# A dense relation layer moved beside a scatter in a graph network kernel

## The chip, the cores and the metric

The kernel runs on one core of a Trainium2 chip. The metric is the device time of one launch in microseconds; the time before is the median of 3 runs.

## What is computed

Four graph layers follow each other on 100,000 nodes of 64 features and 50,000 edges sorted by destination, each with a residual and a layer norm. Each has a part that only nodes reached by an edge need and a dense part for the nodes that no edge reaches:

```python
x = _layernorm(x + L0(x, edge_index, ...))      # graph convolution, two rounds
x = _layernorm(x + L1(x, src, dst, ...))        # attention; without edges: x @ res_W + res_b
x = _layernorm(x + L2(x, edge_attr_64, ...))    # relations; without edges h_nb = 0:
#   out = leaky_relu((nfeat + h_nb) @ res_fc_w.T) + leaky_relu(nfeat * h_nb @ res_fc2_w.T)
x = _layernorm(x + L3(x, src, dst, ...))        # update: mlp([nodes, aggregated])
```

## The kernel before

Nodes are worked in 98 blocks of 1024 (128 partitions by 8 rows), edges ("slots") in 98 blocks of 512. A table in HBM holds slots first and nodes behind them; `x1_table`, `x2_table` and `x3_table` hold the result of the layers. What a node without edges needs is a chain of dense layers over all nodes, attention, relations, update, which the class `Nodes` writes. It is independent of the work on edges, so each dense layer is put beside a stage of the edge work. The stages run one after the other, each in a block of its own with a barrier behind it:

- `own_phase`: gathers each edge's own row (GpSimd), and the dense first layer.
- `slot_phase` (the slot stage): GpSimd writes 392 pieces of `slot_info` into `node_table` with indirect DMAs (L1064) and waits for nothing; beside it the dense attention layer, 98 blocks.
- `first_conv_phase`: 4 gathers a block (L1243), scaling, transposes (L1297), a scan along the edges, a projection (L1304, L1306) and a convolution (L1313); beside it the dense relation layer, 98 blocks.
- `second_conv_phase`: 4 gathers a block (L1424), transposes (L1467), a scan, a sum (L1478, L1480) and its norm; beside it the dense update layer, 98 blocks, whose rows go to the output.
- `attention_phase`, `relation_phase`, `message_phase`: the edge work of the other layers, with no dense layer beside them. The last has 4 gathers (L2380) and 4 scatters a block on GpSimd.

A dense block in `Nodes` goes through these steps: `load` (SP, six buffers, waits until the block six before is transposed), `turn` (TensorE, four transposes, L783, waits for the copy of the block before), `copy` (ScalarE, L861), for relations and update `project` (TensorE, L797 or L794) and `bend` (ScalarE), then `sum_up` (TensorE: L837 and L841 for attention, L845 and L847 for relations, L837, L850 and L853 for update), `squares` (ScalarE, L887), `powers` (VectorE, L914), `roots` (ScalarE, L894), `invert` and `scale_rows` (VectorE), and `store` (SP).

The order on each engine is written by hand: `over_turns` takes a list of stages with their lags, and in turn t each engine issues, in the order of the list, stage (t - lag) of each. An engine waits in order, so what stands behind a waiting instruction waits with it. A TensorE fp32 matmul appears in the profile as two records, a transpose as one.

```python
def over_turns(*stages):
    for turn in range(max(lag + blocks for _, lag, blocks in stages)):
        for stage, lag, blocks in stages:
            if 0 <= turn - lag < blocks:
                stage(turn - lag)
```

## Time and profile before

| | |
|---|---|
| median of 3 runs | 7181.63 us (7180.82 to 7210.08) |
| the profiled execution's own time | 7214.96 us |
| its span | 7213.2 us, mean granted TensorE clock 0.764 |
| TensorE matmul busy | 5373.8 us, 75% |
| VectorE busy | 3019.9 us, 42% |
| ScalarE busy | 1930.0 us, 27% |
| GpSimd busy | 3025.0 us, 42% |

Busy shares are means over seven stages with different limits. The span is that from the first to the last instruction; the execution's own time is the one to set a sum against. PE is TensorE's matmuls, PEld its weight loads, DVE VectorE, ACT ScalarE, POOL GpSimd, SP the engine that issues the plain DMAs. The ends of matmuls are modelled, so when a matmul was really done shows in who waits for it. The granted clock is a share of 2.4 GHz, and is either 1 or 0.5 at any time.

### The profile page before, as it was taken

Reading aid. Unit: us, or ns where it says so; the run is one execution under the profiler, and the core shown is the slowest. Engines: PE = TensorE matmul, PEld = TensorE weight load, DVE = VectorE, ACT = ScalarE, POOL = GpSimd, SP = SyncE. Lnnn points to the kernel's source line nnn. Section 1 sums busy time; section 2 is a strip of 40 time slices with the busy share of each in tenths; the row PEclk is TensorE's granted clock in tenths of the full one; section 3 lists DMA queues with packets and bytes.
Section 4 is the critical chain, followed back from the end, with each engine's and each line's share of the span. In section 5 each row is a group of like instructions: output and inputs, shape, how many; then the busy total and the mean of one; then the engine's idle time right before and its main releaser. Section 6 shows DMA issues by size and latency. Waiting matters only on the chain. (4 is left out here: it accounts for less than half of the span.)

```text
span 7213.2 us, 79067 instructions
## 1 busy us (share of the span) xinstructions
PE 5373.8 (75%) x24847; PEld 3452.0 (48%) x24847; DVE 3019.9 (42%) x5947; ACT 1930.0 (27%) x3627; POOL 3025.0 (42%) x3150
## 2 busy tenths in 40 slices
PE   3888700165888889995578848999999987777776
PEld 2656500144666667773255634444454444444443
DVE  4333300033555535553345526666666642222222
ACT  1333300032333333331111102333343431112121
POOL 2444477501554444445455131222222104666665
PEclk9877755566999989997666559788787857777777
DMA  3666500144666645553344223233232202222221
GB/s 105 191 192 190 163 16 16 28 122 115 168 172 170 156 124 139 137 139 71 71 93 93 64 49 86 72 74 74 72 79 68 68 22 61 52 51 51 52 59 27
DMA packets 1238916, 676.24 MB, mean 94 GB/s; under 512 B 1021942, under 2 KB 1054989, under 8 KB 1238504
## 3 DMA queue, kind: packets, MB, share of 16 engines
q1 hardware_dynamic: 1138152, 582.13, 30.1%
q0 software_dynamic: 100352, 89.06, 6.6%
q8 instruction: 205, 3.36, 0.2%
q14 instruction: 207, 1.70, 0.1%
HBM read 410.58 MB, written 263.03 MB: 93 GB/s over the span
## 5 line engine op out<-in xcount | busy, mean ns | idle before, releaser
L914 DVE TENSOR_REDUCE n_power<-n_square 128x8 f32<-128x512 f32 x392 | 268.9, 686 | 1675.8 <-issue 1069.3
L2075 POOL DMA_INDIRECT r_got<-x_table,slot_idx x392 | 376.9, 961 | 1299.6 <-DVE r_rows L2270 1022.0
L1243 POOL DMA_INDIRECT a_got<-node_table,src_idx x392 | 371.3, 947 | 721.1 <-POOLq L1059 371.3
L887 ACT ACTIVATE n_square<-n_sum_t 128x512 f32<-128x512 f32 x392 | 234.1, 597 | 1317.5 <-remote 567.6
L1424 POOL DMA_INDIRECT b_rows<-h_table,slot_idx x392 | 369.7, 943 | 430.8 <-PE b_rows_t L1467 302.3
L2380 POOL DMA_INDIRECT m_rows<-x_table,slot_idx x392 | 376.7, 961 | 395.8 <-POOLq L2065 276.7
L2388 POOL DMA_INDIRECT out_dram<-s_res,put_out x392 | 390.0, 995 | 338.7 <-DVE s_res L1181 213.2
L952 POOL DMA_INDIRECT o_rows<-in_x_dram,dst_idx x392 | 372.4, 950 | 378.7 <-DVE o_rooted L1032 271.4
L1866 POOL DMA_INDIRECT t_got<-x_table,slot_idx x392 | 372.8, 951 | 362.3 <-DVE t_rows L1984 207.3
L837 PE MATMUL n_sum_t<-res_wide,ones 3*128 3x512 bf16 x98 | 49.7, 507 | 613.0 <-issue 424.5
L2167 PE MATMUL r_source_t<-r_masked,rel_pair 64*128 64x512 f32 x980 | 487.8, 644 | 0.0
L2169 PE MATMUL r_own_t<-r_masked,rel_pair 64*128 64x512 f32 x980 | 487.6, 644 | 0.0
L1141 ACT ACTIVATE s_square<-s_sum_t 128x256 f32<-128x256 f32 x392 | 149.3, 381 | 1246.1 <-remote 523.4
L1064 POOL DMA_INDIRECT node_table<-slot_info,put_slot x392 | 391.1, 998 | 163.5 <-issue 134.0
L2515 DVE TENSOR_TENSOR_SCAN m_both<-m_keep,m_both,m_rows_t 128x512 f32<-128x512 bf16 x97 | 124.1, 1279 | 792.7 <-remote 440.9
L2297 DVE SCALAR_TENSOR_TENSOR r_masked<-r_half,r_both_t 128x512 f32<-128x512 bf16 x490 | 301.2, 681 | 97.8 <-PE r_both_t L2152 69.0
L783 PE MATMUL n_turned_t<-ident,n_rows 128*128 128x128 f32 x1568 | 293.9, 320 | 44.3 <-DMA n_rows<-x_table 33.0
L837 PEld LDWEIGHTS n_sum_t<-res_wide,ones 3*128 3x128 bf16 x98 | 9.4, 96 | 646.3 <-issue 430.5
L861 ACT ACTIVATE n_turned_s<-n_turned_t 128x512 f32<-128x512 f32 x392 | 231.0, 589 | 272.6 <-remote 159.2
L2167 PEld LDWEIGHTS r_source_t<-r_masked,rel_pair 64*128 64x128 f32 x980 | 194.9, 209 | 226.2 <-issue 184.1
L1147 DVE TENSOR_REDUCE s_power<-s_square 128x4 f32<-128x256 f32 x392 | 162.5, 415 | 325.7 <-ACT s_square L1141 262.4
L783 PEld LDWEIGHTS n_turned_t<-ident,n_rows 128*128 128x128 f32 x1568 | 220.5, 166 | 146.7 <-issue 102.1
(362 smaller groups left out, 12834.4 us busy)
## 6 DMA issues: line engine op xcount, KB each, us to landing
n_rows<-x_table SPq DMA_DIRECT2D x294, 256.0 KB
x_table<-n_res SPq DMA_DIRECT2D x196, 256.0 KB
node_table<-n_wide SPq DMA_DIRECT2D x98, 272.0 KB
x_table<-n_res SPq DMA_DIRECT2D x98, 260.0 KB
h_table<-n_conv SPq DMA_DIRECT2D x98, 256.0 KB
x_table<-s_res SPq DMA_DIRECT2D x196, 128.0 KB
r_feats<-in_edge_attr_dram SPq DMA_DIRECT2D x390, 64.0 KB
n_rows<-in_x_dram SPq DMA_DIRECT2D x97, 256.0 KB
```

The costliest lines, as they stand in the source:

```text
L783: last = nc.tensor.transpose(self.turned_t[:, q * P:(q + 1) * P], self.rows[:, n % AHEAD, 2 * q:2 * q + 2, :].rearrange("p j d -> p (j d)" ...
L952: nc.gpsimd.indirect_dma_start(out=rows[:, n % 4, t, :], out_offset=None, in_=x, in_offset=bass.IndirectOffsetOnAxis(ap=dst_idx[:, n * TIL ...
L1064: nc.gpsimd.indirect_dma_start(out=units, out_offset=bass.IndirectOffsetOnAxis(ap=put_slot[:, k:k + 1], axis=0), in_=slot_info[:, k, :], i ...
L1243: nc.gpsimd.indirect_dma_start(out=got[:, n % 4, t, :], out_offset=None, in_=node_table, in_offset=bass.IndirectOffsetOnAxis(ap=src_idx[:, ...
L1424: nc.gpsimd.indirect_dma_start(out=rows[:, n % 4, t, 0:D], out_offset=None, in_=h_table, in_offset=bass.IndirectOffsetOnAxis(ap=slot_idx[: ...
L1866: nc.gpsimd.indirect_dma_start(out=got[:, n % RING, t, :], out_offset=None, in_=x1_table, in_offset=bass.IndirectOffsetOnAxis(ap=slot_idx[ ...
L2075: nc.gpsimd.indirect_dma_start(out=got[:, n % RING, t, :], out_offset=None, in_=x2_table, in_offset=bass.IndirectOffsetOnAxis(ap=slot_idx[ ...
L2167: nc.tensor.matmul(source_t[:, :], rel_pair[0:D, k, :], masked[0:D, n % 2, k, :], start=(k == 0), stop=(k == PAIRS - 1), skip_group_check= ...
L2169: last = nc.tensor.matmul(own_t[:, :], rel_pair[D:P, k, :], masked[D:P, n % 2, k, :], start=False, stop=(k == PAIRS - 1), skip_group_check ...
L2297: nc.vector.scalar_tensor_tensor(out=masked[:, n % 2, k, :], in0=half[:, n % 3, :], scalar=float(k), in1=both_t[:, :], op0=ALU.is_equal, o ...
L2380: nc.gpsimd.indirect_dma_start(out=rows[:, n % 4, t, 0:D], out_offset=None, in_=x3_table, in_offset=bass.IndirectOffsetOnAxis(ap=slot_idx[ ...
L2388: nc.gpsimd.indirect_dma_start(out=out, out_offset=bass.IndirectOffsetOnAxis(ap=put_out[:, n * TILES + t:n * TILES + t + 1], axis=0), in_= ...
```

## The change

The dense relation layer moves from the first convolution into the slot stage, as a second object of `Nodes` named `later` that transposes the attention layer's result rows straight from their buffer in SBUF; its loads from `x2_table` are gone. The dense update layer is halved: blocks 0 to 48 run in the first convolution, 49 to 97 in the second, one block every second turn, with one sum buffer in PSUM. In both convolutions the scan buffer goes from two to three deep, and the edge work behind the scan runs one turn later. The second convolution gets a second buffer for the transposed rows.

```diff
         def turn(self, pe, n):
-            pe.wait_ge(self.loaded[n], self.loaded.done(n))
+            if self.source is None:
+                pe.wait_ge(self.loaded[n], self.loaded.done(n))
+                rows = self.rows[:, n % AHEAD]
+            else:
+                pe.wait_ge(self.source.ready[n], self.source.ready.done(n))
+                rows = self.source.res[:, n % 4]
...
         def scale_rows(self, dve, n):
...
+            if self.reader is not None:
+                if n >= 4:
+                    dve.wait_ge(self.reader.turned[n - 4], self.reader.turned.done(n - 4))
...
     def slot_phase():
             nodes = Nodes(c, "attention")
+            later = Nodes(c, "relations", source=nodes)
...
-                    over_turns((store, AHEAD + 2, BLOCKS), (load, 0, BLOCKS))
+                    over_turns((store_later, AHEAD + 5, BLOCKS), (store, AHEAD + 2, BLOCKS), (load, 0, BLOCKS))
...
-                    over_turns((sum_up, 1, BLOCKS), (turn, 0, BLOCKS))
+                    over_turns((sum_up, 1, BLOCKS), (turn, 0, BLOCKS), (sum_later, 4, BLOCKS), (turn_later, 2, BLOCKS),
+                               (project_later, 3, BLOCKS))
...
-                    over_turns((squares, 1, BLOCKS), (roots, 1, BLOCKS), (copy, 0, BLOCKS))
+                    over_turns((copy, 0, BLOCKS), (squares, 1, BLOCKS), (copy_later, 2, BLOCKS), (squares_later, 4, BLOCKS), (roots, 1, BLOCKS),
+                               (roots_later, 4, BLOCKS), (bend_later, 3, BLOCKS))
...
-                    over_turns((powers, 1, BLOCKS), (invert, 1, BLOCKS), (scale_rows, 1, BLOCKS))
+                    over_turns((powers, 1, BLOCKS), (powers_later, 4, BLOCKS), (invert, 1, BLOCKS), (scale_rows, 1, BLOCKS),
+                               (invert_later, 4, BLOCKS), (scale_later, 4, BLOCKS))
...
+    def every(turns, stage):
+
+        def at_turn(n):
+            if n % turns == 0:
+                stage(n // turns)
+        return at_turn
+
+    EARLIER = BLOCKS // 2
+
     def first_conv_phase():
-            nodes = Nodes(c, "relations")
+            nodes = Nodes(c, "update", 0, EARLIER, sums=1)
...
-            scan = sb(c, "a_scan", [P, 2, EDGE_BLOCK])
+            scan = sb(c, "a_scan", [P, 3, EDGE_BLOCK])
...
-                    over_turns((sum_nodes, 2, BLOCKS), (convolve, 3, BLOCKS), (project_nodes, 1, BLOCKS), (turn, 1, BLOCKS),
-                               (turn_nodes, 0, BLOCKS), (project, 2, BLOCKS))
+                    over_turns((every(2, sum_nodes), 2, BLOCKS), (project, 3, BLOCKS), (every(2, project_nodes), 1, BLOCKS), (convolve, 4, BLOCKS), (turn, 1, BLOCKS),
+                               (every(2, turn_nodes), 0, BLOCKS))
...
     def second_conv_phase():
-            nodes = Nodes(c, "update")
+            nodes = Nodes(c, "update", EARLIER, BLOCKS - EARLIER, sums=1)
...
-            scan = sb(c, "b_scan", [P, 2, EDGE_BLOCK])
-            rows_t = pb(c, "b_rows_t", [P, EDGE_BLOCK])
+            scan = sb(c, "b_scan", [P, 3, EDGE_BLOCK])
+            rows_t = [pb(c, f"b_rows_t{h}", [P, EDGE_BLOCK]) for h in range(2)]
...
-                    over_turns((sum_nodes, 2, BLOCKS), (add_up, 2, BLOCKS), (project_nodes, 1, BLOCKS), (turn, 1, BLOCKS),
-                               (turn_nodes, 0, BLOCKS))
+                    over_turns((every(2, sum_nodes), 2, BLOCKS), (add_up, 3, BLOCKS), (every(2, project_nodes), 1, BLOCKS), (turn, 1, BLOCKS),
+                               (every(2, turn_nodes), 0, BLOCKS))
```

ScalarE, VectorE and SP have the matching lists: the dense update steps at every second turn, the edge steps behind the scan one turn later.

TensorE in the slot stage, one turn and the start of the next, before (the `n_` names are the attention layer's, `ident` the unit matrix for transposes):

```order
L837 MATMUL n_sum_t_2<-res_wide,ones_0 128x512
L841 MATMUL n_sum_t_2<-res_pair,n_turned_s 128x128 x4
L783 MATMUL n_turned_t<-ident,n_rows 128x128 x4
L837 MATMUL n_sum_t_2<-res_wide,ones_0 128x512
L841 MATMUL n_sum_t_2<-res_pair,n_turned_s 128x128 x4
```

and with the change (the `q_` names are the relation layer's):

```order
L850 MATMUL n_sum_t_2<-res_wide,ones_0 128x512
L854 MATMUL n_sum_t_2<-res_pair,n_turned_s 128x128 x4
L796 MATMUL n_turned_t<-ident,n_rows 128x128 x4
L858 MATMUL q_sum_t_2<-slope_pair,q_turned_s 128x128
L860 MATMUL q_sum_t_2<-bent_pair,q_hidden 128x128
...
L796 MATMUL q_turned_t<-ident,n_res 128x128 x4
L810 MATMUL q_hidden_t<-q_turned_s,fc_pair 128x512
L850 MATMUL n_sum_t_2<-res_wide,ones_0 128x512
```

A turn has grown from 9 matmuls and transposes to 22: the relation layer's sum (eight), transposes (four) and projection (one) stand behind the attention layer's transposes.

ScalarE in the slot stage, one turn with the change:

```order
L874 ACTIVATE n_turned_s<-n_turned_t 128x512
L900 ACTIVATE n_square<-n_sum_t_2 128x512
L874 ACTIVATE q_turned_s<-q_turned_t 128x512
L900 ACTIVATE q_square<-q_sum_t_2 128x512
L907 ACTIVATE n_deviation<-n_power,eps 128x8
L907 ACTIVATE q_deviation<-q_power,eps 128x8
L894 ACTIVATE q_hidden<-q_hidden_t 128x512
```

Before, a turn was the square, the root and the copy of the attention layer; the copy now stands ahead, and the bend of the relation layer, on which the next turn's later sum waits, stands last.

## Rows read from the trace of the kernel before

In rows 1 a number in brackets behind a busy time is the count of instructions.

**Rows 1.** Windows view: us; PE, PEld, DVE, ACT, POOL busy (x); PEclk, DMA share, GB/s.

```profile
889.00:1399.00 510.00, 50.79 (x195) 38.47 (x195) 22.13 (x42) 21.51 (x43) 379.38 (x381) 0.51 0.08 17
1422.00:1770.00 348.00, 215.84 (x1049) 163.09 (x1049) 128.00 (x243) 112.04 (x243) 0.00 (x0) 0.71 0.44 119
1810.00:2480.00 670.00, 573.40 (x3319) 429.87 (x3318) 352.10 (x717) 231.42 (x448) 338.30 (x358) 0.93 0.68 169
2570.00:3290.00 720.00, 693.12 (x4487) 524.67 (x4485) 361.75 (x824) 265.51 (x548) 345.34 (x367) 0.96 0.53 134
6000.00:7150.00 1150.00, 850.37 (x3190) 490.16 (x3187) 302.40 (x463) 227.95 (x465) 719.23 (x735) 0.77 0.21 50
```

**Rows 2.** Source view, GpSimd lines: count, ns min/median/max, first and last start us.

```profile
L1064 POOL DMA_INDIRECT node_table<-slot_info,put_slot x392: 981/982/1280, 874.0 to 1398.1; - x196
...
L1243 POOL DMA_INDIRECT a_got<-node_table,src_idx x392: 938/944/1189, 1770.4 to 2490.6; - x196
...
L1424 POOL DMA_INDIRECT b_rows<-h_table,slot_idx x392: 938/944/957, 2528.5 to 3291.1; - x196
...
L2380 POOL DMA_INDIRECT m_rows<-x_table,slot_idx x392: 940/947/1001, 5980.3 to 7166.1; - x196
```

**Rows 3.** Timeline under the scatter: start us, us, instruction, idle before and its releaser.

```profile
1207.86 0.60 PE L837 MATMUL n_sum_t<-res_wide,ones 3*128 3x512 bf16 x1 [33.05 <-issue]
...
1208.39 2.08 PE L841 MATMUL n_sum_t<-res_pair,n_turned_s 128*128 128x128 f32 x8
...
1210.26 1.06 PE L783 MATMUL n_turned_t<-ident,n_rows 128*128 128x128 f32 x4
...
1232.52 0.60 ACT L887 ACTIVATE n_square<-n_sum_t 128x512 f32<-128x512 f32 x1 [24.71 <-remote]
...
1233.15 0.69 DVE L914 TENSOR_REDUCE n_power<-n_square 128x8 f32<-128x512 f32 x1 [34.53 <-issue]
1233.88 0.30 ACT L894 ACTIVATE n_deviation<-n_power,eps 128x8 f32<-128x8 f32 x1 [0.76 <-issue]
...
1243.72 0.60 ACT L861 ACTIVATE n_turned_s<-n_turned_t 128x512 f32<-128x512 f32 x1 [9.55 <-remote]
```

**Rows 4.** Timeline of the slot stage behind the scatter, TensorE at 2.4 GHz.

```profile
1431.31 0.39 PE L837 MATMUL n_sum_t<-res_wide,ones 3*128 3x512 bf16 x1 [1.79 <-ACT n_turned_s L861]
...
1432.62 0.60 PE L783 MATMUL n_turned_t<-ident,n_rows 128*128 128x128 f32 x4
```

**Rows 5.** Timeline of the first convolution, TensorE, one turn.

```profile
2113.31 1.10 PE L1313 MATMUL a_conv_t<-w_cen,a_hidden 128*128 128x64 f32 x8
...
2114.25 1.08 PE L797 MATMUL n_hidden_t<-n_turned_s,fc_pair 128*128 128x512 f32 x2
...
2115.17 0.60 PE L1297 MATMUL a_rows_t<-ident,a_rows 128*128 128x128 f32 x4
...
2116.14 0.38 PE L1304 MATMUL a_hidden_t<-a_root,split 9*128 9x512 bf16 x1
...
2117.41 0.39 PE L845 MATMUL n_sum_t<-slope_pair,n_turned_s 128*128 128x128 f32 x2
...
2119.20 0.98 PE L1313 MATMUL a_conv_t<-w_cen,a_hidden 128*128 128x64 f32 x7
```

**Rows 6.** Timeline of the second convolution, TensorE and GpSimd.

```profile
2905.72 0.38 PE L837 MATMUL n_sum_t<-ub_wide,ones 3*128 3x512 bf16 x1 [0.30 <-issue]
...
2907.76 0.94 POOL L1424 DMA_INDIRECT b_rows<-h_table,slot_idx  x1 [0.30 <-issue]
...
2908.86 0.20 PE L1478 MATMUL s_sum_t<-split,b_root 9*128 9x65 bf16 x1
...
2910.84 1.13 PE L794 MATMUL n_hidden_t<-n_turned_s,u_w 64*128 64x512 f32 x4
...
2911.90 0.66 PE L1467 MATMUL b_rows_t<-ident,b_rows 128*128 128x128 f32 x4
...
2912.83 0.94 POOL L1424 DMA_INDIRECT b_rows<-h_table,slot_idx  x1 [2.88 <-PE b_rows_t L1467]
```

More of the change, by code:

```diff
@@ L698, in build, with __init__ @@
     class Nodes:
-        def __init__(self, c, layer):
-            self.layer = layer
+        def __init__(self, c, layer, first=0, blocks=BLOCKS, source=None, sums=2):
+            self.layer, self.first, self.blocks, self.source, self.reader = layer, first, blocks, source, None
+            if source is not None:
+                source.reader = self
+            tag, of = ("n", "n_") if source is None else ("q", "")
+            of_sums = of or "s_"
             gcn, mlp = layer == "gcn", layer in ("gcn", "update")
-            self.gcn, self.mlp = gcn, mlp
+            self.gcn, self.mlp, self.sum_count = gcn, mlp, sums
@@ L714, in __init__ @@
-            self.sum_t = [pb(c, f"n_sum_t{h}", [P, 2, 512] if gcn else [P, 512]) for h in range(2)]
+            if source is None:
+                self.rows = sb(c, "n_rows", [P, AHEAD, ROWS, D])
+                self.loaded = sig.landing("n_loaded", 1, AHEAD, blocks)
+            self.turned_s = sb(c, f"{tag}_turned_s", [P, 4, 512])
+            self.square = sb(c, f"{tag}_square", [P, 2, ROWS, D])
+            self.power = sb(c, f"{tag}_power", [P, 2, ROWS])
+            self.deviation = sb(c, f"{tag}_deviation", [P, 2, ROWS])
@@ L749, in load @@
             else:
-                table = {"attention": x1_table, "relations": x2_table, "update": x3_table}[self.layer]
-                sp.dma_start(self.rows[:, n % AHEAD], of_nodes(table, n)[:, :, 0:D]).then_inc(self.loaded[n], 16)
+                table = {"attention": x1_table, "update": x3_table}[self.layer]
+                sp.dma_start(self.rows[:, n % AHEAD], of_nodes(table, self.first + n)[:, :, 0:D]).then_inc(self.loaded[n], 16)
         def store_table(self, sp, n):
@@ L1098, in roots, with copy_later, bend_later, squares_later @@
                         nodes.roots(act, n)
-                    over_turns((squares, 1, BLOCKS), (roots, 1, BLOCKS), (copy, 0, BLOCKS))
+                    def copy_later(n):
+                        later.copy(act, n)
+                    def bend_later(n):
+                        later.bend(act, n)
+                    def squares_later(n):
+                        later.squares(act, n)
+                    def roots_later(n):
+                        later.roots(act, n)
+                    over_turns((copy, 0, BLOCKS), (squares, 1, BLOCKS), (copy_later, 2, BLOCKS), (squares_later, 4, BLOCKS), (roots, 1, BLOCKS),
+                               (roots_later, 4, BLOCKS), (bend_later, 3, BLOCKS))
                 @block.vector
@@ L1281, in store_nodes @@
                         nodes.store(sp, n)
[L1282 removed]
+                    over_turns((every(2, store_nodes), 7, BLOCKS), (store, 8, BLOCKS), (load, 0, BLOCKS), (every(2, load_nodes), 0, BLOCKS), (load_rooted, 3, BLOCKS),
                                (by_groups(load_flags), 0, BLOCKS))
@@ L1305, in project @@
                         pe.wait_ge(scanned[n], scanned.done(n))
-                        nc.tensor.matmul(hidden_t[:, :], w1_2[:, :], scan[:, n % 2, :], start=False, stop=True).then_inc(projected[n], 1)
+                        nc.tensor.matmul(hidden_t[:, :], w1_2[:, :], scan[:, n % 3, :], start=False, stop=True).then_inc(projected[n], 1)
                     def convolve(n):
@@ L1453, in store_nodes @@
                         nodes.store(sp, n)
-                    over_turns((store_nodes, 7, BLOCKS), (store, 7, BLOCKS), (load, 0, BLOCKS), (load_nodes, 0, BLOCKS),
+                    over_turns((every(2, store_nodes), 7, BLOCKS), (store, 8, BLOCKS), (load, 0, BLOCKS), (every(2, load_nodes), 0, BLOCKS),
                                (by_groups(load_flags), 0, BLOCKS))
@@ L1479, in add_up @@
                                              skip_group_check=True)
-                            last = nc.tensor.matmul(to[:, t, :], scan[:, n % 2, k], cen2[:, :], start=False, stop=True,
+                            last = nc.tensor.matmul(to[:, t, :], scan[:, n % 3, k], cen2[:, :], start=False, stop=True,
                                                     skip_group_check=True)
```

107 lines of the change are left out of this document (59 added, 48 removed).

## The prediction

> **What bounds the kernel now.** The kernel runs in seven stages, each closed by a barrier, so I read it stage by stage. The windows view comes first [rows 1], with the first and last gather or scatter of each stage beside it [rows 2], then the timeline inside the stages the change touches [rows 3 to 6]. All sums are made against the profiled execution, 7214.96 us with a span of 7213.2 us. The median of the runs is 33.3 us lower, and I subtract that at the end.
>
> The slot stage lasts from 874.0 to 1770.4 us, 896 us [rows 2]. The scatter that GpSimd does ends at 1398.1. The dense attention layer should run beside it, 98 blocks of three VectorE instructions each. But between 1422 and 1770 VectorE still runs 243 of them [rows 1], which is 81 blocks. So only 17 blocks were done in the 548 us before. The stage is scatter, then dense layer, one after the other. The rows say why. In one turn under the scatter TensorE starts the sum at 1207.86 and the transposes at 1210.26, as usual. Yet ScalarE, waiting for the sum, starts only at 1232.52, and for the transposes at 1243.72 [rows 3]. ScalarE and VectorE then follow each other in hundredths of a us. Only what TensorE signals is late, by 22 to 32 us. TensorE completes 195 matmul records in the 510 us from 889 to 1399 [rows 1]: one per 2.6 us, 13 to a turn (1 + 8 + 4 [rows 3]), at a granted clock of 0.51, which is the 1.2 GHz level. Without the scatter a turn takes 348 / 81 = 4.3 us.
>
> The first convolution takes 1770.4 to 2528.5 us. In its steady part there are 358 gathers, four to a block, so 89.5 turns in 670 us, 7.49 us each. TensorE is 86% busy at clock 0.93 [rows 1]. The second takes 720 / (367 / 4) = 7.85 us a turn. TensorE is busy 693.12 us of 720, so it is bound by TensorE. GpSimd is at 5.0 us a turn in both: 0.94 us per gather and 0.30 between them [rows 6].
>
> **The change part by part.**
>
> *Slot stage.* Per block the relation layer adds four transposes, a projection and a sum of eight matmuls. The last two print two records for each matmul [rows 5], so that is 4 + 2 + 16 = 22 TensorE records, and a turn then has 35. If what holds TensorE back goes by records, the scatter covers 195 / 35 = 5.6 turns behind the first two, 8 in all. The bounds of this term are 17 turns, if the delay goes by the turn as now, and 5, if each added wait adds one of its own; with the price of a turn below they move the stage by -49 and +16 us. I take 8, since sum (9 records, 24.7 us) and transposes (4, 11.2 us) come out at the same time per record [rows 3]. VectorE's new wait, for the reader's transposes of four blocks ago, finds them two turns old. If it did hold VectorE, the attention layer's scaling and what is queued behind it would wait, and the reader with them; I cost it at nothing.
>
> What remains is 102 - 8 = 94 turns (98 and a lag of 4) with no scatter beside them. A turn on TensorE at the high clock is: attention sum 1.31 (1431.31 to 1432.62 [rows 4]), transposes twice 0.49 (2115.17 to 2116.14 holds two sets), relation sum 1.79 (2117.41 to 2119.20) and projection 0.92 (2114.25 to 2115.17 [rows 5]), together 5.0 us. The longest loop through the other engines starts at the later layer's sum, which waits for its bend: sum 1.79, transposes 0.49, copy 0.60, squares 0.60, VectorE's sum of squares 0.69, roots 0.30, bend 0.60 [rows 3], 5.07 us and seven handovers of some 0.03. So 5.3 us, and both chains agree. ScalarE has 5 x 0.60 + 2 x 0.30 = 3.6 us of work a turn and VectorE 6 x 0.53 = 3.2 (128.00 us for 243 instructions [rows 1]): neither binds. I take 5.4, for the cold start behind the scatter: 94 x 5.4 = 508 us, the stage ends at 1930 in place of 1770, **+160 us**. SP issues three transfers of 256 KB a turn instead of two. That is 148 GB/s at 5.3 us, where the first convolution moves 169 GB/s [rows 1]: nothing. SP's order (later store, store, load) puts the later store ahead of a load that waits for TensorE anyway.
>
> *First convolution.* TensorE's turn is 5.89 us (2113.31 to 2119.20 [rows 5]). The relation layer in it is 1.79 + 0.49 + 0.92 = 3.20 us. The update layer costs 3.14 for its sum (2905.72 to 2908.86), 1.06 for its projection (2910.84 to 2911.90) [rows 6] and 0.49, together 4.69 us, but every second turn only, 2.35. The turn's TensorE work goes from 5.89 to 5.04 us. The 1.6 us above it (7.49 less 5.89) I take as nearly unchanged: 6.5 us. Bounds: 5.3, TensorE and GpSimd with nothing above them, and 7.2, where the rest grows. 98 x 0.99 = **-97 us**. The three-deep scan buffer and the convolve one turn later remove a wait of TensorE on VectorE that this order could hide already, and are in that 6.5.
>
> *Second convolution.* TensorE goes from 7.55 us (693.12 / 91.75) to 5.2, just above GpSimd's 5.0. What the turn becomes then no row of this stage shows. The nearest is the message stage, which GpSimd bounds: 735 instructions in 1150 us, eight to a block, are 12.5 us a turn, though GpSimd needs 8 x (0.98 + 0.30) = 10.2 and TensorE is busy 9.3 [rows 1]. That is 22% above GpSimd's need. 5.0 x 1.22 = 6.1; I take 6.2 us, 98 x 1.65 = **-162 us**. Bounds: 5.3 and 7.0. The second transposed-rows buffer is in it.
>
> The relation layer's 98 loads of 256 KB vanish, since it reads the attention layer's rows in SBUF; with half the update layer in its place the first convolution has 49 loads and 49 stores fewer on SP's queue, where DMA engines are 68% busy [rows 1]. TensorE and the gathers set the pace there, so I cost that at nothing.
>
> Sum: 160 - 97 - 162 = -99 us. 7215 - 99 = 7116 us, and as a median **7085 us**, 1.3% less.
>
> **A rule against the row.** Row first: under the scatter TensorE's signals come 22 to 32 us late [rows 3]. The Trainium skill (SBUF — State Buffer, "Reading the diagram" in its section on the two sides of the memory) says that inside the engines' side only the port pair that VectorE and GpSimd share causes contention, and that TensorE and ScalarE never wait for anyone. By that rule TensorE would keep its 5.3 us a turn under the scatter. The trace disagrees here, and I go by the trace; the rule's outcome is the third rival.
>
> **The rivals.**
>
> 1. *The clock stays low in the slot stage; slower.* From 1422 to 1770 the granted clock is 0.71 on average [rows 1], a mix of 1.2 and 2.4 GHz. A turn at 1.2 GHz is 1.83 times as long (sum 2.40 us [rows 3] against 1.31 [rows 4]), 9.2 us. At the same mix, 42% of the time high, a turn takes 1 / (0.42 / 5.3 + 0.58 / 9.2) = 7.0 us, and the stage ends 313 us later than now: +54 us, 7236 us; wholly at 1.2 GHz +258. It decides from 6.5 us a turn. The median would be 7203 or, at 1.2 GHz throughout, above 7400 us. Against it: where TensorE is 96% busy the clock is 0.96 and where 86% it is 0.93 [rows 1], and it would be about 94% busy here. Chance 0.12.
> 2. *The convolutions run free.* With one deeper buffer each the 1.6 us goes too, and both take 5.3 us a turn: -215 and -250 with +160 are -305 us, 6876 us. For it: in the second stage next to nothing stands above TensorE's work now. Against it: GpSimd still pauses 2.88 us a turn there [rows 6], and the message stage shows what is left when it doesn't. Chance 0.17.
> 3. *The scatter does cover the layer.* 102 turns of 5.3 us are 541 us, less than the 548 to 1422. The stage would end some 337 us sooner, and with -259 from the others the time is 6586 us. Rows 3 speak against it. Chance 0.02.
> 4. *The delay moves into the convolutions; slower.* With GpSimd pausing less, TensorE's signals come late there as under the scatter, and 7.2 and 7.0 us a turn remain: -28 - 83 + 160 = +49 us, 7231 us. It decides when the two stages together save less than 160 us. Chance 0.11.
>
> **How the numbers follow.** The forecast has 0.58. Its own range, from a slot turn of 5.2 to 6.0 and convolution turns of 6.1 to 6.9 and 5.7 to 6.8, is 7000 to 7175 us. A measurement of this kernel can tell about 0.5%, 36 us, from no change. Faster by more: 0.49 of the forecast's 0.58, rivals 2 and 3, and a little of rivals 1 and 4: 0.69. Within: 0.08 of the forecast and 0.07 of rivals 1 and 4: 0.15. Slower: 0.16. For 8 times in 10 the range takes the forecast, half of rival 2 and the milder part of rivals 1 and 4: 6900 to 7240 us.
>
> **What would show it.** In the changed profile the scatter still takes about 525 us and only 6 to 12 turns of the slot stage end before it does. Behind it turns of 5.2 to 6 us follow at a clock above 0.9. The first gather of the first convolution starts near 1930 us. The gathers of the two convolutions then take about 640 us each with the pauses at their starts, 6.5 and 6.2 us a turn. It is wrong if more than 20 turns end under the scatter, if the slot stage behind it runs at a clock under 0.8, or if a convolution's turn is outside 5.7 to 6.9 us.

## The result and the profile after

The changed kernel takes 7391.3 us (median of 4 runs, 7385.6 to 7398.3) beside 7184.8 for the kernel before, run next to it: 1.027 times as long, with a 95% interval of 1.024 to 1.030. The forecast was 7085 us, and its range ended at 7240. The profiled execution took 7398.33 us, its span 7396.5.

The GpSimd lines in the source view, which answer to [rows 2], bound the stages (count, ns of one, first and last start).

```profile
L1081 POOL DMA_INDIRECT node_table<-slot_info,put_slot x392: 982/985/1976, 883.0 to 1406.3; - x196
...
L1306 POOL DMA_INDIRECT a_got<-node_table,src_idx x392: 941/947/1207, 1924.4 to 2660.7; - x196
...
L1487 POOL DMA_INDIRECT b_rows<-h_table,slot_idx x392: 941/947/957, 2695.6 to 3502.8; - x196
...
L1929 POOL DMA_INDIRECT t_got<-x_table,slot_idx x392: 942/947/1928, 3545.4 to 4231.3; - x196
```

From first start to first start, the slot stage went from 896 to 1041 us (+145), the first convolution from 758 to 771 (+13), the second from 803 to 850 (+47). The stages that the change leaves alone move by +9, -22 and -9. That makes the 183 us between the two spans. So the slot stage cost what it was forecast to cost, and neither convolution gave anything back.

The windows view of the same stretches, answering to [rows 1] (us; PE, PEld, DVE, ACT, POOL busy and count; granted clock, DMA share, GB/s):

```profile
883.00:1406.00 523.00, 68.36 (x241) 48.74 (x241) 17.32 (x34) 20.46 (x43) 394.65 (x391) 0.52 0.08 15
1430.00:1920.00 490.00, 476.76 (x3189) 364.79 (x3189) 273.72 (x552) 288.41 (x643) 0.00 (x0) 0.99 0.50 144
1964.00:2614.00 650.00, 587.49 (x2675) 404.69 (x2674) 269.98 (x546) 155.41 (x252) 325.53 (x340) 0.74 0.56 131
2737.00:3496.00 759.00, 749.60 (x2924) 566.05 (x2924) 295.30 (x675) 165.50 (x360) 340.50 (x360) 0.51 0.40 94
```

Under the scatter VectorE runs 34 instructions, six to a turn: 5.7 turns. Behind it 552 make 92 turns in 490 us, 5.33 us each at clock 0.99. The first convolution takes 650 / (340 / 4) = 7.65 us a turn, and its clock is 0.74 where it was 0.93. The second takes 759 / (360 / 4) = 8.43 us, at 0.51 where it was 0.96: TensorE runs there at 1.2 GHz throughout and is 99% busy. The timeline of the second convolution shows that it is its own bound:

```profile
3002.54 0.60 PE L850 MATMUL n_sum_t<-ub_wide,ones 3*128 3x512 bf16 x1 [0.17 <-ACT n_hidden L891]
3002.64 0.94 POOL L1487 DMA_INDIRECT b_rows<-h_table,slot_idx  x1 [2.33 <-PE b_rows_t L1530]
...
3008.49 0.60 ACT L900 ACTIVATE n_square<-n_sum_t 128x512 f32<-128x512 f32 x1 [6.00 <-PE n_sum_t L866]
...
3012.70 0.95 POOL L1487 DMA_INDIRECT b_rows<-h_table,slot_idx  x1 [5.36 <-PE b_rows_t L1530]
...
3016.33 2.08 PE L807 MATMUL n_hidden_t<-n_turned_s,u_w 64*128 64x512 f32 x4
```

Everyone waits for TensorE, GpSimd 2.33 and 5.36 us in two turns. L807's projection takes 2.08 us where it takes 1.13 at 2.4 GHz.

In the first convolution TensorE's signals come late besides. In this timeline GpSimd issues eight gathers in a row, from 2099.50 to 2109.59, of which the last three stand here:

```profile
2106.13 1.00 PE L1376 MATMUL a_conv_t<-w_cen,a_hidden 128*128 128x64 f32 x8
2106.14 0.95 POOL L1306 DMA_INDIRECT a_got<-node_table,src_idx  x1 [0.30 <-issue]
...
2107.40 0.95 POOL L1306 DMA_INDIRECT a_got<-node_table,src_idx  x1 [0.30 <-issue]
2107.41 0.60 PE L796 MATMUL n_turned_t<-ident,n_rows 128*128 128x128 f32 x4
...
2108.65 0.94 POOL L1306 DMA_INDIRECT a_got<-node_table,src_idx  x1 [0.30 <-issue]
...
2110.95 0.42 DVE L1441 TENSOR_TENSOR a_conv<-a_conv_t,inv_last 128x256 f32<-128x256 f32 x1 [2.97 <-remote]
2111.07 0.60 ACT L874 ACTIVATE n_turned_s<-n_turned_t 128x512 f32<-128x512 f32 x1 [2.27 <-remote]
```

The convolution matmuls end at 2107.13 and the transposes at 2108.01, but VectorE and ScalarE start on them only 3.8 and 3.1 us later, when GpSimd's last gather has ended. Under the scatter the same thing lasts longer. The last transpose starts at 1206.90, and the four are copied at 1295.12.

```profile
1166.20 0.87 PE L796 MATMUL q_turned_t<-ident,n_res 128*128 128x128 f32 x4
...
1196.99 0.60 ACT L874 ACTIVATE n_turned_s<-n_turned_t 128x512 f32<-128x512 f32 x1 [34.41 <-remote]
...
1206.90 0.37 PE L796 MATMUL n_turned_t<-ident,n_rows 128*128 128x128 f32 x1 [2.43 <-issue]
...
1253.12 0.60 ACT L874 ACTIVATE q_turned_s<-q_turned_t 128x512 f32<-128x512 f32 x1 [55.05 <-remote]
...
1295.12 0.60 ACT L874 ACTIVATE n_turned_s<-n_turned_t 128x512 f32<-128x512 f32 x1 [34.40 <-remote]
```

From the end of the transposes, 1207.27, that is 88 us. ScalarE stood waiting for this very signal during the last 34.4 of them; until 1253.12 it waited for the signal before it in its order, of the later layer's transposes that ended at 1167.07, 86 us earlier. From one copy of the attention layer's transposes to the next, 1196.99 to 1295.12, is one turn of 98.1 us for 35 TensorE records, 2.8 us each. Before the change the sum's 9 records came 24.7 us apart and the transposes' 4 came 11.2 us apart [rows 3], 2.7 and 2.8 us each.

### The profile page after: what moved, and what is told of

Read it like the earlier page. It is cut to its first block and busy times, and to the rows that moved or that the text cites. A ratio compares the mean times of both kernels' runs of the same rounds, so it can differ in the third digit from the quotient of the medians.

```text
span 7396.5 us, 78949 instructions
## 1 busy us (share of the span) xinstructions
PE 5705.2 (77%) x24847; PEld 3668.2 (50%) x24847; DVE 3021.5 (41%) x5947; ACT 1926.4 (26%) x3627; POOL 3039.4 (41%) x3150
## 5 line engine op out<-in xcount | busy, mean ns | idle before, releaser
L927 DVE TENSOR_REDUCE n_power<-n_square 128x8 f32<-128x512 f32 x294 | 201.7, 686 | 1153.7 <-ACT n_square L900 737.4
L900 ACT ACTIVATE n_square<-n_sum_t 128x512 f32<-128x512 f32 x294 | 175.2, 596 | 817.6 <-PE n_sum_t L866 399.9
L858 PE MATMUL q_sum_t<-slope_pair,q_turned_s 128*128 128x128 f32 x784 | 168.1, 298 | 265.7 <-issue 214.0
L866 PEld LDWEIGHTS n_sum_t<-u_w_cen,n_hidden 128*128 128x128 f32 x1568 | 329.7, 291 | 0.0
L866 PE MATMUL n_sum_t<-u_w_cen,n_hidden 128*128 128x64 f32 x1568 | 328.0, 355 | 0.0
L874 ACT ACTIVATE n_turned_s<-n_turned_t 128x512 f32<-128x512 f32 x294 | 175.2, 596 | 445.7 <-remote 287.8
L796 PE MATMUL n_turned_t<-ident,n_rows 128*128 128x128 f32 x1176 | 234.5, 330 | 69.4 <-issue 30.4
```

The lines of the kernel that those rows point to most:

```text
L866: last = nc.tensor.matmul(to[:, q * P + odd * D:q * P + odd * D + D], hidden[:, odd, pair(q)], u_w2_cen[:, :], start=False, stop=True, ski ...
```

## The experiments

Three things were to be told apart: TensorE's clock (the halved layer leaves it at 1.2 GHz), the order of the convolutions (deeper buffers, a turn later, one turn heavy and one light), and TensorE's late signals (held up while GpSimd issues indirect transfers back to back). Each group of experiments ran on one chip, beside the kernel before, and the chips differ: the kernel before takes 7202 us in the first group, 7279 and 7287 in the next two, 5996 and 6001 in the last two. So totals are compared as ratios within a group. A total within 2% of the kernel before's counts as level here; the readings rest on the stages. The stages below go from first start to first start, as above; clock is the granted clock in that stage.

| kernel | ratio (95%) | slot | first conv., clock | second conv., clock |
|---|---|---|---|---|
| changed | 1.027 (1.024-1.030) | 1041 | 771, 0.73 | 850, 0.51 |
| e1 layer moved only | 1.001 (1.000-1.003) | 1040 | 631, 0.60 | 809, 0.92 |
| e2 second in old order | 1.039 (1.036-1.042) | 1040 | 773, 0.76 | 953, 0.52 |
| e3 more TensorE work | 0.997 (0.995-1.000) | 1040 | 773, 0.76 | 638, 0.92 |
| e4 pause after 4 | 0.983 (0.980-0.986) | 730 | 766, 0.75 | 853, 0.51 |
| e5 update all in first | 1.017 (1.010-1.024) | 1041 | 1023, 0.81 | 592, 0.50 |
| e6 pause after 8, work | 0.969 (0.966-0.972) | 754 | 797, 0.88 | 713, 0.78 |
| e7 before, pause after 4 | 0.975 (0.971-0.978) | 706 | 782, 0.92 | 831, 0.91 |
| e8 short pauses | 0.980 (0.977-0.984) | 716 | 774, 0.75 | 850, 0.51 |
| e9 tied | 0.963 (0.960-0.965) | 678 | 738, 0.77 | 859, 0.50 |
| e10 tied, work | 0.935 (0.932-0.938) | 674 | 717, 0.86 | 642, 0.94 |
| e11 before, tied | 0.944 (0.942-0.946) | 603 | 684, 0.94 | 813, 0.92 |
| e12 memsets between | 0.973 (0.971-0.974) | 695 | 777, 0.75 | 830, 0.53 |
| e13 tied, first in old order | 1.007 (1.005-1.010) | 531 | 565, 0.99 | 842, 0.51 |
| e14 work in light turns | 0.968 (0.965-0.971) | 531 | 614, 0.98 | 578, 0.98 |
| e15 work in heavy turns | 0.974 (0.972-0.977) | 533 | 606, 0.98 | 617, 0.98 |
| e16 changed again | 0.994 (0.991-0.997) | 531 | 523, 0.97 | 851, 0.50 |
| e17 tied, light work | 0.963 (0.962-0.965) | 530 | 574, 0.97 | 578, 0.98 |
| e18 before tied again | 1.001 (1.000-1.002) | 519 | 590, 0.98 | 805, 0.91 |

**First group.** *e1*: `Nodes` and its stages out of the first convolution, the second as in the kernel before.

> The relation layer stays beside the scatter as in the changed kernel; the first convolution has no dense layer, in its new order; the second is that of the kernel before, with the whole update layer. Clock theory (in both convolutions TensorE's clock falls to the 1.2 GHz level when its work is cut, and its work at that level then sets the turn): the second convolution is back at 803 us with a clock of 0.93 or more, since its TensorE work is back at 7.55 us a turn; the first has 2.7 us of TensorE work at 2.4 GHz and 4.9 at 1.2, so GpSimd's 5.0 us bound it at either clock, 5.3 to 6 us a turn, 540 to 620 us: in all 7391 - 47 - (150 to 230) = 7115 to 7195 us. Order theory (the new order of the convolutions, a turn later and with deeper buffers, costs what was lost): the second is back at 803 us as well, but the first stays near 700 us or more though its TensorE has little to do: 7270 us or more.

The second convolution is back at 809 us and clock 0.92. The first takes 6.1 us a turn, above the 5.0 us of GpSimd: 631 us, just outside the range. The total is 19 us above the clock theory's and 56 us below the order theory's. In the first convolution late signals are left: its waits view from 1964 to 2450 us (us in total, times, longest) has

```profile
ACT a_hidden L1393 <- remote: 234.7, 29, 10.7
```

*e2* and *e3*:

```diff
 e2: second_conv_phase of the kernel before, with
-            nodes = Nodes(c, "update")
+            nodes = Nodes(c, "update", EARLIER, BLOCKS - EARLIER)
 and every(2, ...) around its stages
 e3, second_conv_phase, turn:
-                        for t in range(TILES):
+                        for t in list(range(TILES)) * 3:
```

> The changed kernel with the second convolution's order, its two scan buffers and its one transposed-rows buffer of the kernel before; the update layer stays halved, every second turn. Clock theory: the TensorE work is the same, the clock stays near 0.5 and the stage at 850 us, within 25 us: 7365 to 7415 us. Order theory (the deeper pipeline put TensorE's work in an order with a new chain of waits): the stage falls by 100 us or more with a clock above 0.9, 7290 us or less.

> The changed kernel, but TensorE makes each of the four transposes of the second convolution's turn three times, to the same place: the same result, and some 1.0 us more TensorE work a turn at 2.4 GHz (0.49 us for a set of four), 1.8 at 1.2 GHz. Clock theory: with more to do TensorE keeps the high clock; a turn takes 5.2 + 1.0 = 6.2 to 6.7 us in place of 8.4, the stage 630 to 680 us in place of 850, in all 7170 to 7220 us. Order theory, or a clock that falls for another reason than too little work: the added work only adds, 98 x 1.0 to 98 x 1.8, 7490 to 7570 us.

e3 settles the second convolution. With 784 more matmul records there its windows row reads

```profile
2679.60:3317.40 637.80, 598.89 (x3969) 474.97 (x3969) 320.62 (x736) 173.61 (x392) 369.67 (x392) 0.92 0.53 124
```

in place of 3185 records in 850 us at 0.51: more work took 212 us away, and the whole kernel is level with the one before (0.997). In e2 the clock stays at 0.52, so the new order is not why it fell. e1 and e2 have the same order in this stage and differ in the dense layer alone, whole or half of it:

```profile
2678.60:3631.70 953.10, 809.72 (x3185) 606.33 (x3185) 322.06 (x736) 179.34 (x392) 369.62 (x393) 0.52 0.35 83
```

in e2, and in e1

```profile
2529.20:3338.20 809.00, 766.99 (x4802) 573.66 (x4802) 388.27 (x883) 286.48 (x588) 370.61 (x393) 0.92 0.51 129
```

Twice the dense layer takes 144 us less. So the update layer's own matmuls raise the clock as well as repeated transposes do. But in e2 the stage grew by 103 us over the changed kernel's where I expected no change: at the low clock the new order is worth a microsecond a turn.

*e4*, in the slot stage:

```diff
                             oob_is_err=False).then_inc(placed, 16)
+                        if k % 4 == 3 and k >= 0:
+                            pool.wait_ge(placed, 16 * (k + 1 - 0))
```

> The changed kernel, but in the slot stage GpSimd waits after every fourth scatter until all those issued have landed. The scatter then takes some 2 to 3 us more per four, 98 x 2.5 = 245 us more than 523. Issue theory (TensorE's completions come late because GpSimd issues its indirect transfers back to back; in a pause they come at once): each pause lets the signals through, the layers advance about one turn per pause, and most of the 98 turns are done when the scatter ends; the stage takes 770 to 900 us in place of 1041, in all 7120 to 7250 us. Rival (it is the traffic of the scatter, or the number of scatters, that holds TensorE's signals up, pauses or not): turns under the scatter stay below 15, the stage becomes 1041 + 245 - 40 = 1250 us, in all 7600 us.

The scatter takes 199 us longer, from 872.8 to 1595.3, and the stage is 311 us shorter: the next stage starts 8 us after the last scatter does, with all blocks done. Late signals are what kept the layers from running beside it.

**Second group.** e5 has the whole update layer in the first convolution, none in the second; e6 pauses after every eighth scatter and makes the transposes three times in the first convolution, twice in the second; e7 puts e4's pause into the kernel before; e8 lets only two scatters be under way:

```diff
-                            oob_is_err=False).then_inc(placed, 16)
+                            oob_is_err=False).then_inc(placed[k % 2], 16)
+                        if k >= 1:
+                            pool.wait_ge(placed[(k - 1) % 2], 16 * ((k - 1) // 2 + 1))
...
```

> The changed kernel, with the whole update layer every turn in the first convolution and no dense layer in the second, both in the new order. Clock theory: the first has 2.7 + 4.7 = 7.4 us of TensorE work a turn, about what the second convolution had in the kernel before, so its clock is 0.92 or more and its turn 7.7 to 8.1 us: a stage of 755 to 800 us where it is 771 with half of that layer. The second has 2.9 us at 2.4 GHz, 5.2 at 1.2, and is paced by GpSimd's gathers at either clock, as the first convolution was without a dense layer (6.1 us a turn at a clock of 0.61): 555 to 635 us in place of 850. In all 7100 to 7210 us. Rival (the new order itself lets the clock fall in the first convolution): its clock stays at 0.75, 7.4 us of work then take 9.5 or more, and the stage takes over 900 us, the whole 7250 us or more.

> Three edits of the changed kernel, each in a stage of its own: the scatter pauses after every eighth until all have landed; the first convolution makes its transposes three times, to the same place; the second makes them twice. Slot stage: with half of the pauses the scatter takes some 625 us where it took 722 with a pause after every fourth, and the layers, 5.3 us a turn, need 541; if eight issues in a row hold the signals no longer than the next pause lets through, 630 to 700 us; if the layers fall behind the scatter, 740 us or more. First convolution: 1.0 us more work a turn keeps the clock above 0.9 by the clock theory, 6.3 to 6.9 us a turn and a stage of 630 to 700 us in place of 771; if it only adds, 850 us. Second: half a microsecond more work instead of one is enough by the clock theory if TensorE is still some 95% busy, 590 to 640 us; if it is too little, the stage stays near 850. In all 6600 to 6800 us by the clock theory throughout, 7000 or more if the added work only adds.

> The kernel before, with the scatter's pause after every fourth and nothing else. Issue theory: the attention layer alone needs 4.3 us a turn and gets 7.4 us per four scatters, so it ends with the scatter: the slot stage takes some 730 us in place of 896, the whole 7035 us (7010 to 7060). The changed kernel with the same pauses took 7083 us. Rival (the pauses helped there for a reason that lies in the added layer): no gain or a loss of up to 200 us.

> The changed kernel, but GpSimd never has more than two scatters under way: after each it waits for the one before to have landed, on one of two semaphores in turn. A scatter lands some 3.4 us after its start and two are issued in 2.6, so each is followed by a pause of some 0.5 us, about as much pause in all (some 200 us) as with a wait after every fourth, in pieces a fifth as long. If TensorE's signals come through in any pause, the stage is 720 to 780 us, the whole 7070 to 7130 us. If they need a pause of some length, or come only when nothing of the scatter is under way, few turns are done beside the scatter, which ends 200 us later: a stage of 1150 us or more, 7480 us or more.

e5 missed in the first convolution: 1023 us where the clock theory had 755 to 800, 7420 us in all, as its rival (a low clock from the new order: over 900 us, 7250 or more), though the clock was 0.81 and not the rival's 0.75. So e5 does not clear the new order. There is a second cause that I had overlooked: with one sum buffer (`sums=1`) and a layer every turn, each sum waits for the scaling of the one before. Its waits view has

```profile
ACT n_square L900 <- issue: 327.7, 87, 5.5
...
PE n_sum_t L850 <- DVE n_res L943: 83.1, 90, 1.1
```

(us in total, times, longest): nearly every sum waits for `n_res`, 83 us in all, which is less than the 223 us that are missing; the rest stays open. In its second convolution TensorE has little work, the clock is 0.50 and the stage 592 us, as expected: a low clock costs nothing where GpSimd binds. e6 missed twice. Its clock in the first convolution rose to 0.88 and yet the stage grew from 774 us (e8, same chip) to 797, so on that chip the clock alone does not bind there; and half a microsecond of added work left the second half way, at 0.78. With half the pauses the layers fall behind the scatter: 754 us, more than with pauses twice as many. e7 and e8 came out close to what was expected, in the slot stage 24 and 4 us better: the kernel before gains from pauses too, and short pauses do about as well as long ones. e7's total, 7094 us, lies above its range, on a chip where the kernel before takes 94 us more than was assumed. In e8 GpSimd is idle 0.83 us before a scatter on the mean, unevenly, where it is 0.30 without pauses.

**Third group.** e9 ties GpSimd to TensorE in place of pausing it; e10 adds transposes (twice in the first convolution, three times in the second); e11 is the kernel before with the same ties, less the one to the later layer; e12 has no waits but, after every fourth scatter, four clears of a scratch tile.

```diff
 e9, slot_phase, ahead of the scatter:
+                        if k % 4 == 0 and k >= 4:
+                            pool.wait_ge(nodes.turned[k // 4 - 1], nodes.turned.done(k // 4 - 1))
+                        if k % 4 == 2 and k >= 14:
+                            pool.wait_ge(later.turned[k // 4 - 3], later.turned.done(k // 4 - 3))
 e9, first_conv_phase, gather:
+                        if n >= 2:
+                            pool.wait_ge(turned[n - 2], turned.done(n - 2))
```

> The changed kernel with GpSimd tied to TensorE's progress in two stages. Slot stage: before every fourth scatter it waits for the attention layer's transposes of the step before, and two scatters later for the later layer's transposes of the same step. First convolution: before the four gathers of a block it waits for the transposes two blocks back, so that it can no longer issue eight or more in a row. Issue theory (what holds TensorE's signals up are runs of indirect transfers without a pause; a pause as short as the wait for the signal is enough): the slot stage takes the longer of the scatter's 523 us with its pauses and 102 turns, 600 to 700 us in place of 1041; the first convolution loses the waits behind its runs, 6.3 to 7.2 us a turn, 640 to 730 us in place of 771. In all 6950 to 7020 us on a chip where the changed kernel takes 7391. Rival for the first convolution (its time is set by the order of the stages and the uneven turns): the shorter look-ahead takes nothing away, 770 us or more.

> The tied kernel with more TensorE work: transposes twice in the first convolution and three times in the second, to the same place. First convolution: if with the ties its turn is set by TensorE at a low clock, 0.5 us more work raises the clock and the turn falls to 6.0 to 6.8 us, 620 to 690 us; if the signals still bind, it changes by less than 20 us against the tied kernel. Second: 638 us in place of 850, as where it had this alone. Slot stage as in the tied kernel. In all some 210 to 290 us less than the tied kernel.

> The kernel before with the same ties, where the slot stage waits for the attention layer's transposes alone: what the two layouts are worth once GpSimd no longer runs ahead. Issue theory: slot stage 580 to 680 us in place of 896 (the attention layer's turn takes 4.3 us alone), the first convolution 6.5 to 7.3 us a turn, 660 to 730 us in place of 758, the second as before, 803. In all 6870 to 6990 us on a chip where the kernel before takes 7185. If it is level with or ahead of the tied changed kernel, moving the layer to the scatter is worth nothing as long as the second convolution's clock stays low.

> The changed kernel, but after every fourth scatter GpSimd clears a scratch tile of 128 x 512 four times in place of a wait: it is as busy as before, some 2 to 2.5 us of each 7.5 with work that issues no transfer. If it is the issuing of indirect transfers that holds TensorE's signals up, they come through during the clears as in a wait: a slot stage of 720 to 780 us, as with pauses. If GpSimd must be idle for them, the scatter ends 200 us later with as few turns done beside it: a stage of 1200 us or more.

e12 shows what holds the signals up. In this timeline GpSimd pauses no more than before, and the copy of the transposes that ended at 1202.79 starts 1.6 us later, 1.3 us into the clears, in place of tens of us:

```profile
1202.11 0.98 POOL L1082 DMA_INDIRECT node_table<-slot_info,put_slot  x1 [0.31 <-issue]
1202.19 0.60 PE L796 MATMUL q_turned_t<-ident,n_res 128*128 128x128 f32 x4
...
1203.08 1.94 POOL L1090 MEMSET idle<- 128x512 f32 x4
...
1204.40 0.60 ACT L874 ACTIVATE q_turned_s<-q_turned_t 128x512 f32<-128x512 f32 x1 [2.99 <-remote]
...
1205.20 0.98 POOL L1082 DMA_INDIRECT node_table<-slot_info,put_slot  x1 [0.17 <-issue]
```

It is the issuing of indirect transfers without a break, not a busy GpSimd. Nor is it transfers under way. In e8 the transposes that end at 1201.10 are copied at 1201.13, while the third scatter below still waits for the first one to land:

```profile
1199.68 0.98 POOL L1081 DMA_INDIRECT node_table<-slot_info,put_slot  x1 [0.97 <-issue]
...
1201.13 0.60 ACT L874 ACTIVATE q_turned_s<-q_turned_t 128x512 f32<-128x512 f32 x1 [1.41 <-PE q_turned_t L796]
...
1203.48 0.98 POOL L1081 DMA_INDIRECT node_table<-slot_info,put_slot  x1 [1.53 <-DMA node_table<-slot_info,put_slot]
```

The ties are cheaper still, 678 us. They took 39 us from the first convolution (777 in e12, same chip), which at 738 is still 8 us above e9's range. That of the kernel before takes 684 us with them, in place of 758 and 782 in the two runs without them, and is 54 us ahead of the changed one. e10's added work took 21 us more from it, less than expected (717 us, where the clock alone was to give 620 to 690), and 217 us from the second convolution. With ties in both, the added work decides: 0.935 against 0.944. Whether the kernel before would gain from added work was not tried.

**Fourth group.** e13 is e9 with the first convolution in its old order; e14 and e15 have the tied first convolution and, in both, the transposes five times in every second turn:

```diff
-                        for t in range(TILES):
+                        for t in list(range(TILES)) * (1 + 4 * (n % 2 == 0)):
 e15: * (1 + 4 * (n % 2))
```

> The tied kernel with the first convolution's order and its two scan buffers of the kernel before; the update layer stays halved there, every second turn. If the new order is what keeps the tied first convolution at 7.4 us a turn, the stage falls from 738 to 690 us or less, towards the 684 of the tied kernel before. If it is the low clock (0.77) and the two unlike turns, the old order helps nothing: 738 us or, as in the second convolution, up to 100 us more.

> The changed kernel with the first convolution tied as before, and in both convolutions the transposes five times in every second turn, the one without the update layer's sum: 2.0 us more there at 2.4 GHz, 1.0 on the mean of two turns, which makes the two turns alike (5.9 and 6.5 us in the second convolution). If it is the light turn that lets the clock fall, it rises as with three times in every turn: a second convolution of 630 to 660 us, clock above 0.9. If only the amount counts, the same. First convolution: 680 to 740 us with a clock above 0.85.

> As the one before, with the added transposes in the other turns, those with the sum: the same amount of work, the heavy turn 8.5 us and the light one 3.9. If it is the light turn, shorter than what GpSimd needs for its gathers, that lets the clock fall, the second convolution stays at a clock of 0.5 to 0.6 and takes 900 us or more. If only the amount of work counts, it takes 630 to 680 us at a clock above 0.9 like the other. First convolution: over 740 us if the unlike turns matter there, else as in the other.

On this chip no signal of TensorE is late under the scatter (in e13 the transposes that end at 806.08 are copied at 806.11), and even the first stage of all, which no kernel here touches, takes 517 us in place of the 780 of [rows 2]'s kernel (94.1 to 874.0). The second convolution still stays at 0.51 in e13. The same added work raises it to 0.98 whether it goes to the light turns (578 us) or to the heavy ones (617):

```profile
1756.20:2334.50 578.30, 562.65 (x3969) 453.44 (x3969) 317.12 (x736) 169.62 (x392) 369.85 (x393) 0.98 0.58 136
```

and in e15

```profile
1754.50:2371.40 616.90, 567.87 (x3969) 455.55 (x3969) 320.96 (x736) 174.92 (x392) 369.79 (x392) 0.98 0.54 128
```

So the light turn is not what lets the clock fall; uneven turns cost 39 us of their own. The question that e13 was for, the order on a chip with late signals, stays open, since it landed on this one.

**Fifth group.** The changed kernel once more, e10 with e14's added work in the second convolution, and e11 again; the chip is again one without late signals.

> The changed kernel as it is, once more, since the chips differ: on three chips the kernel before takes 7202, 7279 and 7287 us, on a fourth 5996, and there no signal of TensorE came late. On a chip of the first kind: 2.4 to 3.0% slower than the kernel before, a slot stage of 1041 us, the second convolution 850. On one of the second kind: the scatter covers both dense layers, a slot stage of 531 us; the first convolution 565 to 600; the second still 842 at a clock of 0.51, since its clock falls there too: in all some 6020 to 6070 us where the kernel before takes 5996, 0.4 to 1.3% slower.

> The version that the runs point to: GpSimd tied to TensorE's progress in the slot stage and the first convolution, transposes twice in the first convolution, and five times in the light turns of the second. On a chip where signals come late: slot stage 675, first convolution 717, second 620 to 645, in all 0.930 to 0.937 of the kernel before. On a chip where they don't: slot stage 531, first convolution 580 to 600, second 578, some 5790 us, 0.965 of the kernel before.

> The kernel before with the same ties, beside the two others on one chip. Where signals come late: 0.944 of the kernel before, as it was. Where they don't, the ties have nothing to shorten: within 1% of the kernel before.

Under e16's scatter the transposes end at 804.01 and ScalarE has them at 804.04:

```profile
802.99 0.98 POOL L1081 DMA_INDIRECT node_table<-slot_info,put_slot  x1 [0.30 <-issue]
...
803.41 0.60 PE L796 MATMUL q_turned_t<-ident,n_res 128*128 128x128 f32 x4
...
804.04 0.60 ACT L874 ACTIVATE q_turned_s<-q_turned_t 128x512 f32<-128x512 f32 x1 [1.41 <-PE q_turned_t L796]
```

The changed kernel takes 0.6% less here than the one before, where e16's expectation had 0.4 to 1.3% more: the first convolution took 523 us where I expected 565 to 600. Beside e18, which has the kernel before's work, the slot stage costs 12 us more and the second convolution 46, and the first saves 67. Within e16 the two convolutions stand side by side in the windows view:

```profile
1180.00:1640.00 460.00, 460.00 (x2859) 320.27 (x2857) 288.44 (x591) 167.56 (x272) 348.24 (x362) 1.00 0.83 197
1700.00:2480.00 780.00, 772.27 (x2967) 583.05 (x2966) 301.60 (x689) 168.47 (x367) 343.20 (x364) 0.50 0.40 93
```

The first runs 5.08 us a turn at 2.4 GHz, the second 8.57 us at 1.2, and TensorE is 99% busy or more in both. e17 beats both kernels there (0.963), and its sister e10 does on a chip with late signals (0.935).

## Why the prediction was wrong

*Slot stage: right.* I forecast 8 of the 102 turns under the scatter, 5.4 us for each of the 94 behind it and +160 us. VectorE's work makes it 5.7 full turns under the scatter and 92 behind it (the others are the short ones at the start), 5.33 us each, and +145. The first rival, a low clock there, fell at 0.99; its text takes the 33 us off twice, the median of its sum is the 7236 and not 7203. Delay by the record, not by the turn, gave the right count, and that was no luck: 2.7 to 2.8 us a record in both kernels. e4, e8 and e12 show what causes it. The third rival failed on this chip, as [rows 3] said. The rule named beside it (the Trainium skill, SBUF — State Buffer, "Reading the diagram") speaks of engines that wait at the memory's ports. No run here shows such a wait, so the late signals do not refute it; what failed is the step from that rule to 5.3 us a turn under the scatter. On the two chips of the last groups the scatter did cover both layers: the stage took 531 us, about the third rival's 541 for 102 turns. I had no second chip to see it. No chip is known to have been used twice, so that the lateness belongs to the chip, and not to its state at the time, is not shown.

*First convolution: wrong*, by the forecast's own bound of 5.7 to 6.9 us. The step "The 1.6 us above it (7.49 less 5.89) I take as nearly unchanged: 6.5 us", -97 us, measured 7.65 us in its steady part and +13. TensorE's work in a turn went down and what stands above it did not stay: late signals were no constant addition, and the clock fell from 0.93 to 0.74. That is the way of the fourth rival, though past its 7.2 us. e9 shows that a part, 39 us, is GpSimd running ahead. e10's higher clock, 0.86, gave 21 us more, and e6's 0.88 nothing at all, so added work gives back little here. Where nothing is late the stage runs free, 5.08 us a turn in e16, the second rival: 523 us, 67 less than the kernel before's 590 (e18). So the new order costs nothing by itself, and the stage's loss comes only with the late signals. How it divides there between the lateness, the clock and the order is open.

*Second convolution: wrong, and it decides the result.* "I take 6.2 us", -162 us, measured 8.43 and +47. The sum priced TensorE's 5.2 us a turn at 2.4 GHz without asking at which clock it would run. I had a clock rival and put it in the slot stage; the message stage, the row that I took as nearest, ran at 0.77 [rows 1], which should have been a warning. With the 1.83 of the first rival TensorE's 5.2 us would have come to 9.5, above the 7.85 of before: that product was within reach of the rows. It was 8.4: the product is 1.1 us too high, but on the right side of 7.85. At the high clock the stage takes 638 us even with 1.0 us more work (e3), and 578 us on a chip without late signals (e14). That 638 is near the 641 that 803 - 162 gives is chance: the forecast had no added work. e1, e2 and e3 leave the amount of TensorE work as the cause; why the first convolution keeps the high clock in e16 with about as much work a turn, none of them shows.

Costed at nothing, and no stage shows a price for it: VectorE's wait for the reader, SP's three transfers a turn, the loads that vanish.

## What to carry to other kernels

When work is taken from TensorE, price what is left at both clock levels, and read the granted clock of the very stage: if the low level makes TensorE the bound, less work can take longer. A cheap test is to repeat some matmuls that write the same result to the same place; if the stage gets shorter, it was the clock. Where TensorE's signals arrive late beside a stream of indirect transfers, tie the issue of the transfers to TensorE's progress rather than let it run as far ahead as buffers allow. Measure on more than one chip before the layout is chosen.

## What was not expected of the hardware

- TensorE 99% busy at a granted clock of 0.50 for 780 us, and 100% busy at 1.00 in the stage ahead of it: the busy share does not tell which level a stage gets. About 1 us of transposes a turn raised it on both kinds of chip, 0.5 us half way. It need not be transposes: the other half of the update layer did it too (e1 beside e2).
- Completion of TensorE's matmuls reached the other engines up to 88 us late under an unbroken scatter, 3 to 4 us late beside the first convolution's gathers, and not late on two chips. The kernel before takes 7182 to 7287 us on the first sort and about 6000 on the second. On the first it gains 2.5% from pauses (e7) and 5.6% from ties (e11); on the second the ties gain nothing (1.001, e18), and pauses were not tried.
- Under the unbroken scatter the signals come at 2.7 to 2.8 us for each TensorE record. A mean idle time of 0.83 us between scatters (e8), or 1.9 us of memsets after every fourth (e12), is enough to let them through; 0.30 us between all scatters is not.
